# Two-layer cross-attention on one core: softmax sums one step earlier in the second layer, loads moved behind the reciprocals, row maxima over twelve steps, and a new layout of the change of layers

## The reference, cut to what matters

```python
# layer 0: heads 64 wide, no scaling of the logits
h = layernorm(x) * gamma + beta
Q, K, V = h @ Wq, context @ Wk, context @ Wv          # 16 heads of 64
attn = softmax(Q K^T) * 64 ** -0.5
x = x + (attn V) @ Wo + bo
# layer 1: heads 32 wide, rotated and normalised q and k
xn = x * rsqrt(mean(x * x) + eps) * norm_w
q, k, v = xn @ wq, context @ wk, context @ wv         # 16 heads of 32
q, k = rotate(q), rotate(k)
q, k = q / norm(q), k / norm(k)
attn = softmax(q k^T * sqrt(32))
out = x + (attn v) @ wout
```

## Time and profile before

| what | value |
|---|---|
| median of 3 runs | 3298.59 us (3295.31 to 3302.42) |
| the profiled execution's own time | 3303.01 us |
| its span | 3301.2 us |
| TensorE busy | 3101.7 us (94%) |
| VectorE busy | 2367.9 us (72%) |
| ScalarE busy | 1411.3 us (43%) |
| GpSimd busy | 454.2 us (14%) |
| mean granted share of TensorE's clock | 0.983 |

### The profile page before, as it was taken

The page is one execution under the profiler, slowest core; times in us unless marked ns, Lnnn a source line. Parts: engine busy times, 40 slices in busy tenths (PEclk is TensorE's granted clock), DMA queues, the critical chain, the costliest instruction groups (busy, mean ns, idle before and its releaser), DMA issues.

```text
span 3301.2 us, 73709 instructions
## 1 busy us (share of the span) xinstructions
PE 3101.7 (94%) x31708; PEld 1577.5 (48%) x31708; DVE 2367.9 (72%) x2804; ACT 1411.3 (43%) x1728; POOL 454.2 (14%) x221
## 2 busy tenths in 40 slices
PE   6999999899899999989989999999999999999997
PEld 3555555444355555544335455554434455555441
DVE  3677776687777776678777777667877777776887
ACT  1333333456433333355633333335563333334564
POOL 1000002342000000325100000023400000013430
PEclk8999999999999999999999999999999999999999
DMA  3011010201111000011111010101112101010001
GB/s 110 15 25 26 21 25 16 59 21 40 45 51 28 21 25 21 22 51 27 38 48 47 25 28 21 25 15 57 24 40 63 32 21 26 24 25 19 21 16 37
DMA packets 178410, 107.33 MB, mean 33 GB/s; under 512 B 81452, under 2 KB 147116, under 8 KB 178088
## 3 DMA queue, kind: packets, MB, share of 16 engines
q1 hardware_dynamic: 178088, 102.60, 11.8%
HBM read 93.12 MB, written 9.42 MB: 31 GB/s over the span
## 4 chain that ended last, share of the span: by engine, by line
PE 82%; DVE 10%; issue 4%; DMA 2%; ACT 2%; SPq 1%; DVEq 0%; POOL 0%; ACTq 0%; POOLq 0%
PE o_acc L693 19%; PE scores L681 19%; PE work L720 12%; PE work L714 11%; PE work L758 10%; PE work L649 5%; DVE acc L855 4%; PE work L751 2%; PE work L741 2%; DVE tile_max L836 2%; PE work L768 1%; DVE stats L875 1%; PE work L746 1%; DVE sumsq L916 1%; ACT probs L785 1%
## 5 line engine op out<-in xcount | busy, mean ns | idle before, releaser
L785 ACT ACTIVATE probs<-scores 128x1024 f32<-128x1024 f32 x1024 | 996.2, 1023 | 522.4 <-PE scores L681 489.2
L855 DVE TENSOR_TENSOR acc<-acc,probs 128x1024 f32<-128x1024 f32 x768 | 963.5, 1276 | 20.7 <-DVE acc L855 0.9
L836 DVE TENSOR_REDUCE tile_max<-work 128x2 f32<-128x1024 f32 x496 | 606.8, 1223 | 477.3 <-PE work L649 474.3
L693 PE MATMUL o_acc<-probs,v_tok 128*64 128x512 f32 (+1 forms) x4096 | 778.1, 612 | 0.3 <-ACT probs L785 0.3
L970 POOL TENSOR_TENSOR inv<-sumsq,power 128x16 f32<-128x16 f32 x64 | 186.5, 2914 | 2058.9 <-DVE sumsq L918 2058.9
L758 PE MATMUL work<-wo,o_sum 128*32 128x512 f32 (+1 forms) x2072 | 403.6, 608 | 65.4 <-issue 35.3
L681 PE MATMUL scores<-q_high,k_high 32*128 32x512 f16 (+1 forms) x2048 | 309.7, 394 | 25.8 <-ACT probs L785 12.7
L693 PEld LDWEIGHTS o_acc<-probs,v_tok 128*64 128x64 f32 (+1 forms) x4096 | 165.5, 122 | 347.1 <-issue 333.9
L940 DVE TENSOR_TENSOR resid<-work,resid 128x512 f32<-128x512 f32 x384 | 261.3, 684 | 94.1 <-PE work L758 93.9
L681 PE MATMUL scores<-q_high,k_low 32*128 32x512 f16 (+1 forms) x2048 | 303.1, 384 | 0.0
L681 PE MATMUL scores<-q_low,k_high 32*128 32x512 f16 (+1 forms) x2048 | 302.2, 383 | 0.0
(11 more groups left out here) (76 smaller groups left out, 2684.3 us busy)
## 6 DMA issues: line engine op xcount, KB each, us to landing
recip<-rows_dram SPq DMA_DIRECT2D x380, 64.0 KB, 2.2
stage<-in_x_dram SPq DMA_DIRECT2D x8, 1024.0 KB, 7.2
wq<-in_L_xattn_Wq_dram SPq DMA_DIRECT2D x32, 256.0 KB, 2.7
resid<-in_x_dram SPq DMA_DIRECT2D x8, 1024.0 KB, 5.3
wo<-in_L_xattn_Wo_dram SPq DMA_DIRECT2D x32, 256.0 KB, 2.7
out_dram<-resid SPq DMA_DIRECT2D x8, 1024.0 KB, 4.5
wk<-in_L_xattn_Wk_dram SPq DMA_DIRECT2D x32, 192.0 KB, 2.4
wv<-in_L_xattn_Wv_dram SPq DMA_DIRECT2D x32, 192.0 KB, 2.5
```

Of the source, the lines that this page charges most:

```text
L693: mm = pe.matmul(o_acc[h * d:(h + 1) * d, :], v_tok[par][:, kt, h * d:(h + 1) * d], probs[:, unit_slot(t, n, kt, h // 2), h % 2, :], start ...
L785: act.activation(probs[:, no % RING, :, :], scores[:, unit_banks(t, n, kt, u), :], ACT.Exp, scale=(1.0, float(D1) ** 0.5 / QK_SCALE ** 2)[ ...
L836: dve.tensor_reduce(tile_max[:, qt, :, n:n + 1], maxima_banks(e), AX.X, ALU.max, negate=True).then_inc(dve_freed, 1)
L855: dve.tensor_tensor(a[:, heads, :], before, probs[:, unit_slot(t, n, kt, u), :, :], ALU.add).then_inc(add_ok, 1)
```

## The change

In layer 1 `den` moves from the next half's first step to the end of its own half's last step; `recip` stands at the end of the next half's second step where it stood at the start of the third (the same place on VectorE where no maximum follows, but ahead of a step's loads on SP). The next batch's loads move one step down. The eight context tiles go from two a step (four steps) to mostly one a step (steps 1 to 7 of turn 2.1), two of the input's transposes to the last step of turn 2.0. The sixteen maxima of the next batch's first turn are spread over steps 4 to 7 of turn 3.0 and all eight of turn 3.1. At the change of layers `kT` of turn 0 goes one step up, `kr` of turn 1 one (first half) and one step (second half) down, `norm_b` ahead of the additions, and the values' second halves stand together.

```diff
--- before.py
+++ after.py
@@ -111,9 +111,9 @@
     t6, t7, t8, t9 = (b * (TURNS0 + TURNS1) + i for i in (6, 7, 8, 9))
     return {(6, 0): [E("T", t6, 1), E("q", t7, 1), E("v", t7, 0) + E("T", t7, 0), E("v", t7, 1)],
             (7, 0): [[], E("kr", t8, 0), E("kr", t8, 1), []],
-            (6, 1): [E("T", t7, 1), [], [], E("kT", t8, 0, 1) + E("norm_a", (b, 1), 0) + E("kr", t9, 0)],
-            (7, 1): [E("norm_b", (b, 1), 0) + lead("v", t8, 0) + transposed(1, b, 0, 0, 1, 2, 3) + E("v", t8, 0) + E("qr", t8, 0),
-                     E("v", t8, 1) + E("kr", t9, 1), E("qT", t8, 0), []]}[p, n]
+            (6, 1): [E("T", t7, 1), [], E("kT", t8, 0, 1), E("norm_a", (b, 1), 0)],
+            (7, 1): [E("kr", t9, 0) + transposed(1, b, 0, 0, 1, 2, 3) + lead("v", t8, 0) + E("qr", t8, 0),
+                     E("v", t8, 0) + E("v", t8, 1), E("qT", t8, 0) + E("kr", t9, 1), []]}[p, n]
 
 
 def layer1_beside(b, p, n):
@@ -135,11 +135,13 @@
     more = ()
     if b < B - 1:
         nb = b + 1
-        more = {(1, 0): ((1, E("load_x", nb, 0, 1) + E("load_c", nb, *range(C_RING))),),
+        more = {(1, 0): ((2, E("load_x", nb, 0, 1) + E("load_c", nb, *range(C_RING))),),
                 (1, 1): ((5, E("norm_a", (nb, 0), 0)), (6, E("norm_b", (nb, 0), 0))),
-                (2, 1): ((0, E("norm_a", (nb, 0), 1)), (1, context(nb, 0, 1)), (2, context(nb, 2, 3) + transposed(0, nb, 0, 0, 1)),
-                         (2, E("norm_b", (nb, 0), 1)), (3, context(nb, 4, 5) + transposed(0, nb, 0, 2, 3)), (4, context(nb, 6, 7)),
-                         (5, transposed(0, nb, 1, 0, 1)), (6, transposed(0, nb, 1, 2, 3)), (7, lead("k", t12, 0))),
+                (2, 0): ((7, transposed(0, nb, 0, 0, 1)),),
+                (2, 1): ((0, E("norm_a", (nb, 0), 1)), (1, context(nb, 0, 1)), (2, context(nb, 2) + transposed(0, nb, 0, 2, 3)),
+                         (2, E("norm_b", (nb, 0), 1)), (3, context(nb, 3) + transposed(0, nb, 1, 0)), (4, context(nb, 4)),
+                         (5, context(nb, 5) + transposed(0, nb, 1, 1)), (6, context(nb, 6) + transposed(0, nb, 1, 2)),
+                         (7, context(nb, 7) + transposed(0, nb, 1, 3) + lead("k", t12, 0))),
                 (3, 0): ((0, E("k", t12, 0)), (1, E("k", t12, 1)), (2, lead("q", t12, 0)), (3, E("q", t12, 0)), (4, lead("q", t12, 1)),
                          (5, E("q", t12, 1))),
                 (3, 1): ((0, lead("v", t12, 0)), (1, E("v", t12, 0)), (2, lead("v", t12, 1)), (3, E("v", t12, 1)), (4, E("T", t12, 0)),
@@ -157,7 +159,7 @@
         if p < TURNS1 - 1 or b == B - 1:
             return [[]] * 8
         r = rowmaxes(t + 1, 0) + rowmaxes(t + 1, 1)
-        ends = (0, 0, 0, 0, 0, 0, 0, 2, 4, 6, 8, 10, 12, 14, 16, 16, 16)
+        ends = (0, 0, 0, 0, 0, 1, 2, 3, 4, 5, 6, 7, 9, 10, 12, 14, 16)
         return [r[ends[8 * n + i]:ends[8 * n + i + 1]] for i in range(8)]
     if p > 5 and n == 1:
         return [[]] * 4
@@ -173,14 +175,12 @@
     return [r[ends[i]:ends[i + 1]] for i in range(4)]
 
 
-def add_results(half, t, n, beside, maxima):
+def add_results(half, t, n, beside):
 
     b, l, p = TURN[t]
     outs = [Entry("out", t, n * HT + i) for i in range(HT)]
     if len(half) == 8:
-        at = 0 if maxima[0] else len(beside[0])
-        beside[0][at:at] = E("den", t, n)
-        half[2].early += E("recip", t, n)
+        beside[1] += E("recip", t, n)
         half[4].early += E("norm_o", t, n)
         each = 2 if (l, p) == (0, TURNS0 - 1) else 1
         for i in range(HT // each):
@@ -223,8 +223,12 @@
         maxima = maxima_beside(t, n)
         per = KT // n_steps
         half = [Step(t, n, tuple(range(i * per, i * per + per))) for i in range(n_steps)]
+        if j > 0 and l == 1:
+            steps[-1].fill += E("den", *HALVES[j - 1])
+        if (l, p, n) == (0, 7, 1):
+            half[0].early += E("norm_b", (b, 1), 0)
         if j > 0:
-            add_results(half, *HALVES[j - 1], beside, maxima)
+            add_results(half, *HALVES[j - 1], beside)
         if j > 1 and TURN[HALVES[j - 1][0]][1] == 0:
             t0, n0 = HALVES[j - 2]
             if TURN[t0][1] == 0 and (TURN[t0][2], n0) != (7, 0):
```

## The result

| kernel | median us (lowest to highest) | ratio to before, 95% interval |
|---|---|---|
| before, beside it on the same chip, 5 runs | 3302.42 (3295.31 to 3312.44) | |
| changed, 5 runs | 3321.86 (3316.97 to 3326.01) | 1.0055 [1.0039, 1.0071] |

The account below looks back on a forecast made before the run. TensorE's work plus its waits bound the kernel. Terms 32.4 - 11.5 - 7.9 + 2.4 + 2.3 + 0 + 2 gave +19.7 us on the profiled 3303.0; against the median 3318, taken as 3316, range 3291 to 3331.

Parts of the forecast that it names:

- The sums: Ends of turns 0.0, 0.1, 1.1, 2.0: earlier `den` adds 2.4, 2.1, 2.3, 1.3 us a batch; +32.4 us.
- The step that failed: `out` after turn 0.0's end loses its own 1.7 us wait, as TensorE arrives 4 us later; net +2.4 us a batch.
- Rival 2: An earlier `den` ends waits ahead of `out` in turns 0.1, 1.1 and 2.0; 22 us less, 3294; chance 0.2.
- The loads: Turn 1.0: loads moved behind the reciprocals shorten the waits of `out` in three batches; -11.5 us.
- Context: Context tiles, one a step: the 10.3 us of waits for them shrink; -7.9 us.
- Maxima: Turn 3.0 step 4 to the batch's end: +2.4 us over three batches, and +2.3 us in batch 3 for `den`.
- My walk through the last four steps: Batch's end: two maxima a step, 6.0 to 7.3 us a step; stretch from turn 3.0 step 4 takes 67.3 us.
- The change of layers: At the change of layers new waits take the place of old ones; 0, between -4 and +4 us a batch.
- three late things: Change of layers: `kT`'s bank 0.7 us, `xt`'s third bank 2.1 us, `den` behind rotation and two additions 1.9 us.
- The clock: Half-clock stretches behind TensorE's waits: 13 removed, 26 us of cost; some 16 new, +28 us; net +2 us.
- Rival 3: The clock falls behind each new wait, seven stretches more; 12 us more, 3328; chance 0.13.
- Rival 1: VectorE keeps ahead in the last four steps, waits for maxima and their half-clock stretches go; 36 us less, 3280; chance 0.17.

Follow-up runs that it names:

- experiment 1: Changed kernel with `den` back at the end of the next half's first step, all else as changed; 3257.86 us, ratio 0.9868 to before.
- 2: Kernel before with the move of `den` and `recip` alone, loads still ahead of the reciprocals; 3340.08 us, ratio 1.0112 to before.
- 9: Changed kernel with `norm_o` a step earlier, ahead of the fourth step's additions; 3359.24 us, ratio 1.0165 to before.
- 12: Changed kernel with `recip` at the end of the next half's first step and `norm_o` ahead of its fourth step's additions; 3314.93 us, ratio 1.0039 to before.
- 7: Changed kernel with `den` at the start of the next half's first step, about 2 us later; 3267.95 us, ratio 0.9900 to before.
- experiment 3: Kernel before with only the next batch's loads one step down, behind the reciprocals; 3285.40 us, ratio 0.9947 to before.
- 4: Kernel before with the maxima's new places alone, twelve steps instead of nine; 3290.57 us, ratio 0.9968 to before.
- parts 2 to 6: Kernel before with one edit each: sums 1.0112, loads 0.9947, maxima 0.9968, context 0.9987, change of layers 0.9967.
- 11: Changed kernel with the change of layers laid out as before; 3329.03 us, ratio 1.0075 to before.

## Why the prediction was right, and where it wasn't

**The sums.** The mechanism was right, place by place: `acc` hangs on VectorE's own list, TensorE reaches `den` too early, and the wait is as long as the gap between the scores' old start and the last addition (4.5, 2.0, 2.3, 1.3, 1.8 us as in the table above). Experiments 1 and 2 show that this edit alone makes the change a loss; without it the rest gains 1.3%. **The step that failed** is "so `out`'s own wait of 1.7 us ... goes too". I took the 1.7 us in batch 3 for the way over DRAM, because `norm_o` there followed close behind the landing. It was VectorE's place: in the changed kernel nothing had to land, and 1.70 stayed in all four batches, behind two additions and a `norm_o` of 1.76 us; it went in 9 and in 12, where `norm_o` stood ahead of those additions. Net 4.0 us a batch there, not 2.4, so this term was mis-sized by 6.4 us, of which turn 1.1 of batch 3 gave 2.3 back.

**Rival 2**, that the waits are given back at `out`, is refuted for the kernel as changed: its four rows of `out` have 47.2 us, and 44.5 in 1 and 45.5 in 7, where `den` stands later. It holds in part where the loads are not moved: in 2 some 12 us of `out` in turn 1.0 came back. Experiment 12 shows what it would have needed, both `recip` and `norm_o` moved, and that even then the change stays slower than the kernel before. The same two moves with `den` in its old place were not run. My expectation for 9 repeated the error of the failed step with the signs exchanged: one place, turn 1.0, taken for all.

**The loads.** -11.5 us of waiting forecast; `out` in turn 1.0 went from 5.8, 5.0 and 5.9 to 1.7, which is -11.5, and experiment 3 has the idle time down by 12.4.

**Context, maxima, change of layers.** Each was sized too low in gain. Context: the DMA's waits went as forecast; alone the edit is worth 0.13%, 4 us. Maxima: +4.7 us was forecast with `den`'s share in it, about 1.5 x 3 + 2.3 = 6.8, so -2 without it; alone it gave 0.32%, 10 us. My walk through the last four steps made them longer than they are: 65.5 us for the stretch with `den`, against a forecast 67.3. The change of layers: forecast 0 with `den`'s four waits of 1.9 in it, so -8 without; alone it gave 0.33%, 11 us. Its three late things came as forecast (0.5, 2.0, 1.8 us), and they took back less than the waits they replaced. The four gains alone add up to 0.53 + 0.32 + 0.13 + 0.33 = 1.31%, and together, in experiment 1, they are 1.32%.

**The two errors met.** Let the sum be split anew, by whether a wait is `den`'s or not. The forecast waits of `den`, in turns 0.0 to 1.1, at the change of layers and beside the maxima, and in batch 3 of turn 2.0, make 4 x (2.4 + 2.1 + 2.3 + 1.9) + 6.8 + 1.3 = 43 us, and the page shows 46.4 us of idle time between 1 and the changed kernel. All else (loads; context; its bank at the end of turn 2.0, 3 x 1.3; maxima and layers without `den`) was to give -11.5 - 7.9 + 3.9 - 2.1 - 7.6 = -25 us of waiting and gave -35.8. So 11 us too little gain was forecast and 3 us too little loss, and the two errors cancel in part. The forecast was 19.7 us above the profiled execution of before, and the spans differ by 13.9. That the medians differ by 19.4, so nearly by the forecast, is luck: the 5.5 us between the two come from which executions were profiled, and no term of the sum stands for them.

**The clock.** +2 us net was forecast, 26 removed and 28 added. The traces have 22 stretches of half clock before (111.1 us), 15 in experiment 1 (70.4) and 21 in the changed kernel (108.7). TensorE's busy time fell by 13.3 us from before to 1 and rose by 16.6 from 1 to the changed kernel. So in the profiled executions the net was near nothing, as forecast, but both sides were nearly twice too large. The other four executions of the changed kernel had a lower granted share, 0.982 to 0.983, so what the clock costs in its median isn't fixed by this.

I had counted 16 stretches behind the new waits, and there are 12. The seven waits of 2.3 us or more (end of turn 0.0 four times, of turn 1.1 three) each have one, as the two windows above show, and so have the four of 2.0 us ahead of `xt` at the change of layers; of the four of 2.0 us at the end of turn 0.1 one has, of the four of 1.8 at the change of layers and the three of 2.1 ahead of maxima none. The Trainium skill ("TensorE: Matmul & The Clock Gate", What's actually happening) has the default state as the throttled one, which activity releases. That agrees with the direction, and no row contradicts it; but a wait's length alone doesn't decide here. The same wait of 2.0 us at the end of turn 0.1 has a stretch in one batch of four in the changed kernel, in three in 2 and in all four in 12, and of the four of 2.6 us in 7 only one has. What does decide stays open. Rival 3 (every new wait has one) would have given 12 us more, and did not happen.

**Rival 1** (the maxima decide) is refuted by 4: 24.9 of the 35.9 us remain. Its side of the result, faster, was reached in experiment 1 instead, by all the other edits together.

What stays open: the parts 2 to 6 sum to 0.74% less than the change. Half of that, 12.4 us or 0.37%, is the wait of `out` in turn 1.0, which both 2 and 3 remove. In idle time alone the parts sum to -2.2 us where the change has +10.6, a gap of 12.8 that this wait nearly fills. But `den` at the new change of layers, 7.2 us that none of the parts has, should come on top; 11 shows this wait too, and what makes up for it isn't shown.

## What to carry to other kernels

When a producer is moved up in a list that every engine follows in order, ask not when its consumer could start but which instruction of the chain behind it stands still: here the sums left earlier, `recip` and `norm_o` kept their places, and the whole wait was a loss, but for what it hid of the loads' delay while those stood in the way. Where a wait nearly coincides with two limits, a DMA's landing and an engine's place, one that looks like the cause in one batch or half must be read in the others before a term is built on it. And price a bundle of edits one by one: four small gains of 0.1 to 0.5% were hidden here by one loss of 1.9%.

## What the runs showed of the hardware

- VectorE's multiplication `norm_o` took 0.68 us as a rule and 1.76 us where it ran beside GpSimd's addition over 128x512 elements (1468.71 to 1470.41 above), in turn 1.0 of all four batches. VectorE's addition to `resid`, one of whose inputs is in PSUM, kept its 0.68 to 0.69 us in the 24 places where it ran beside the same GpSimd instruction. In experiment 9 `norm_o` stood ahead of that addition and took 0.68 again, while the additions that now lay beside GpSimd took 4.58 us for three, where two take 2.35, and GpSimd's own 2.32 instead of 1.70:

```profile
1479.66 0.68 DVE L868 TENSOR_TENSOR o_sum<-o_sum,recip 128x512 f32<-128x512 f32 x1
1480.26 4.58 DVE L859 TENSOR_TENSOR acc<-acc,probs 128x1024 f32<-128x1024 f32 x3
```

```profile
1481.43 2.32 POOL L976 TENSOR_TENSOR raw_q<-raw_q,turned 128x512 f32<-128x512 f32 x1
```

- A wait of 4.5 us cost TensorE more than its length: three of the four at the end of turn 0.0 had a half-clock stretch of 6.83 us, the fourth one of 3.41. In batch 1 `den` itself took 1.94 us instead of 1.06. The stretches behind the seven waits of 2.3 us or more hold 27.4 us of TensorE's work. At half clock half of that, an estimated 13.7 us, was lost, on top of 25 us of waiting.
- The way of 8 KB over DRAM and back as rows, from `recip` to `norm_o`, is 7.0 us (batch 1, turn 0.1 of experiment 9). It is one transfer out, with 2.8 us from issue to landing in the changed kernel, and behind it four back, with 2.2 us each and 4.2 at most.
